# Routing and expert slots in one instruction stream, with the gate's projection turned

## The reference

```python
x = x + tanh(g_xattn[0]) * xattn(ctx, ctx, layernorm(x), ssm_kernel, D, 8)   # long convolution of k*v, then times q
x = x + tanh(g_ffn[0]) * ffn(layernorm(x), G, gate_w, up_w, down_w, lora_A, lora_B)

# ffn
scores = softmax(x @ G)                       # 8 experts
value, indices = top_k(scores, 2)             # w: weight per token and expert, zero but for two
gated = silu(x @ gate_w[e].T) * (x @ up_w[e].T)
out  = sum_e w[e] * (gated @ down_w[e].T)
out += sum_e w[e] * ((x @ lora_A[e].T) @ lora_B[e].T)
```

## Time and profile before

| what | value |
|---|---|
| median of 3 runs | 1526.3 us |
| the three runs | 1525.24 to 1528.57 us |
| profiled execution, its own time | 1529.94 us |
| profiled execution, its span | 1527.8 us |
| mean granted clock | 0.964 |
| busy: TensorE, VectorE, GpSimd, ScalarE | 93%, 75%, 73%, 51% |

### The profile page before, as it was taken

How to read it: one execution, slowest core, us unless ns; L and a number is a source line. 1 busy time by engine, 2 the same in 40 slices (tenths; PEclk the granted TensorE clock), 3 DMA queues, 4 the chain that set the end, 5 groups by cost and what they waited for, 6 DMA issues and landing times. The chain is left out here.

```text
span 1527.8 us, 34088 instructions
## 1 busy us (share of the span) xinstructions
PE 1417.1 (93%) x10482; PEld 1380.8 (90%) x10483; DVE 1151.5 (75%) x1923; ACT 774.4 (51%) x1359; POOL 1113.6 (73%) x982
## 2 busy tenths in 40 slices
PE   3999999999999999999999999933699999999994
PEld 3999999999999999999999999933699999999994
DVE  2999999999999999999999999948245454444542
ACT  5555665666566665656565666310233343433331
POOL 6998988898898989898989898405155555555552
PEclk9999999999999999999999999955799999999998
DMA  6666676767676767676767676345389999999984
GB/s 198 196 220 221 208 222 208 226 203 234 202 221 205 238 196 228 200 232 202 227 200 226 208 219 214 131 158 125 88 180 271 239 238 239 259 263 219 245 172 79
DMA packets 114343, 315.46 MB, mean 206 GB/s; under 512 B 25152, under 2 KB 25664, under 8 KB 114304
## 3 DMA queue, kind: packets, MB, share of 16 engines
q1 hardware_dynamic: 93728, 239.96, 50.2%
q0 software_dynamic: 20576, 75.04, 22.1%
HBM read 215.66 MB, written 100.86 MB: 207 GB/s over the span
## 5 line engine op out<-in xcount | busy, mean ns | idle before, releaser
L532 DVE TENSOR_REDUCE oT<-z 128x128 f32<-128x1280 f32 x256 | 380.4, 1486 | 7.8
L633 PE MATMUL Y<-kvhi,t_hi 128*128 128x288 f32 x1280 | 383.1, 299 | 0.0
L634 PE MATMUL Y<-kvlo,t_hi 128*128 128x288 f32 x1280 | 378.4, 296 | 0.0
L635 PE MATMUL Y<-kvhi,t_lo 128*128 128x288 f32 x1280 | 377.6, 295 | 0.0
L307 POOL TENSOR_TENSOR kvlo<-kv,kvhi 128x1152 fp32r<-128x1152 f32 x128 | 340.6, 2684 | 0.0
L290 POOL TENSOR_TENSOR kv<-cT 128x768 f32<-128x768 f32 x128 | 238.0, 1859 | 9.3 <-DMA cT<-in_c 9.3
L635 PEld LDWEIGHTS Y<-kvhi,t_lo 128*128 128x128 f32 x1280 | 241.4, 189 | 0.0
L634 PEld LDWEIGHTS Y<-kvlo,t_hi 128*128 128x128 f32 x1280 | 241.3, 189 | 0.0
L633 PEld LDWEIGHTS Y<-kvhi,t_hi 128*128 128x128 f32 x1280 | 241.1, 188 | 0.0
L515 DVE TENSOR_TENSOR z<-Y,qT 128x512 f32<-128x512 f32 x256 | 176.9, 691 | 51.2 <-PE Y L635 42.4
L1230 PE MATMUL GU<-wt_hi,xu_hi 128*128 x568 | 171.5, 302 | 0.0
(11 more groups left out here) (172 smaller groups left out, 3402.8 us busy)
## 6 DMA issues: line engine op xcount, KB each, us to landing
cT<-in_c SPq DMA_DIRECT2D x32, 768.0 KB, 8.0
t_hi<-khi SPq DMA_DIRECT2D x64, 384.0 KB, 3.6
t_lo<-klo SPq DMA_DIRECT2D x64, 384.0 KB, 5.0
u_hi<-kshi SPq DMA_DIRECT2D x64, 320.0 KB, 5.8
u_lo<-kslo SPq DMA_DIRECT2D x64, 320.0 KB, 6.9
x_nat<-in_x SPq DMA_DIRECT2D x32, 512.0 KB, 4.1
out<-x_new SPq DMA_DIRECT2D x32, 512.0 KB, 4.8
normed<-n SPq DMA_DIRECT2D x32, 512.0 KB, 7.5
```

What stands on the lines that cost most here:

```text
L532: nc.vector.tensor_reduce(oT[p][:, 2 * r:2 * r + 2, h * IB:(h + 1) * IB], view(z[s][:], [[ZC, 2], [2, IB], [2 * IB, ZS], [1, 2]]), AX.XY, ...
L633: nc.tensor.matmul(out, w_hi[:, w], m_hi[:, c, :], start=start, stop=False)
L634: nc.tensor.matmul(out, w_hi[:, w], m_lo[:, c, :], start=False, stop=False)
L635: return nc.tensor.matmul(out, w_lo[:, w], m_hi[:, c, :], start=False, stop=stop)
```

## The change

- In `attend` the projection is turned: `ag_parts` (16 columns) is the loaded operand and the tile's high and low parts side by side (`n2_parts`, 256 columns) move, 8 matmuls in place of 16. The result lies on 16 partitions. ScalarE copies 16 x 256 of it into `gated` (zeroed once by VectorE), TensorE transposes it back in two matmuls (`turn`, new, between `shared(i, 1)` and `conv(i, 1, 0)`) into XP's second bank, and VectorE sums four numbers for each logit. `take_lr` moves behind `total(i, p, 0, 3)`.
- In the slots HT is gone; `turn` writes into GU of the slot's parity. This frees a bank, so that the PSUM and SBUF tensors of routing and of slots exist together.
- Routing and slots are one `Block`, one program per engine. In place of the stop come the semaphores `spare_out` and `tables_done`.
- In routing the memsets of `lora_b` and `wt` move from VectorE to GpSimd, those of `shift` to where VectorE waits for the counts. `keep.token` and `keep.dest` are formed before the `need` tables; VectorE then waits until GpSimd has issued two gathers (`first_rows`), and makes the tables. SyncE waits for the weights of expert 0 before it issues those of expert 1, and no longer waits for a memset first.
- `lora_b` gets a semaphore of its own, so TensorE waits for two counts in each slot, both computed from the slot's expert in registers.

```diff
                 def take_small(i):
                     eng.wait_ge(ag_ready, i + 1)
-                        eng.wait_ge(lr_done, i)
-                    nc.scalar.copy(p_small[:], XP[:, E:2 * E]).then_inc(small_done, 1)
+                    if isinstance(i, int) and i < 1:
+                        eng.wait_ge(gated_zero, 1)
+                    else:
+                        eng.wait_ge(turned, i)
+                    nc.scalar.copy(gated[0:2 * E, :], XP[0:2 * E, 0:2 * P]).then_inc(small_done, 1)
...
                 def take_lr(i):
-                    eng.wait_ge(ag_ready, i + 1)
+                    eng.wait_ge(turned, i + 1)
-                    eng.wait_ge(small_done, i + 1)
-                    nc.vector.tensor_tensor(to, XP[:, 0:E], p_small[:], ALU.add).then_inc(lr_done, 1)
+                    nc.vector.tensor_reduce(to, view(XP[:], [[1, E], [P, 2], [E, 2]], HALF), AX.XY, ALU.add).then_inc(lr_done, 1)
...
                     multiply(i, p, 0, 3)
+                    total(i, p, 0, 3)
                     if not (isinstance(i, int) and i < 2):
                         take_lr(i - 2)
-                    total(i, p, 0, 3)
...
                     for c in range(NC):
-                        nc.tensor.matmul(XP[:, 0:2 * E], n2_hi[:, c, :], ag_parts[:, c].rearrange("p o n -> p (o n)"),
-                                         start=c == 0, stop=False)
-                        mm = nc.tensor.matmul(XP[:, 0:E], n2_lo[:, c, :], ag_parts[:, c, 0, :], start=False, stop=c == NC - 1)
+                        mm = nc.tensor.matmul(XP[0:2 * E, 0:2 * P], ag_parts[:, c].rearrange("p o n -> p (o n)"),
+                                              n2_parts[:, c].rearrange("p o n -> p (o n)"), start=c == 0, stop=c == NC - 1)
                     mm.then_inc(ag_ready, 1)
+
+                def turn(i):
+                    eng.wait_ge(small_done, i + 1)
+                    for half in range(2):
+                        mm = nc.tensor.transpose(XP[:, HALF + half * P:HALF + (half + 1) * P],
+                                                 gated[:, half * P:(half + 1) * P], ident[:])
+                    mm.then_inc(turned, 1)
...
                     shared(i, 1)
+                    if not (isinstance(i, int) and i < 2):
+                        turn(i - 2)
                     conv(i, 1, 0)
...
@@ route_tokens, VectorE @@
-                V.memset(weights.lb[:].bitcast(F32), 0.0).then_inc(weights.lb_zero, 1)
-                link(V.memset(wt[:], 0.0))
-                for b in range(NB):
-                    link(V.memset(shift[:, b, :], float(NB - 1 - b)))
...
         link(V.memset(cum[:], 0.0))
+        for b in range(NB):
+            link(V.memset(shift[:, b, :], float(NB - 1 - b)))
         eng.wait_ge(cnt_done, 1)
...
+        eng.wait_ge(idx_done, 1)
+        V.tensor_scalar(keep.token[:], IDX[:, 0:SG], -1.0, 0.0, ALU.add, ALU.max).then_inc(token_done, 1)
+        link(V.tensor_scalar(spare[:], IDX[:, 0:SG], 0.0, number[:, NT:NT + 1], ALU.is_equal, ALU.mult))
+        V.scalar_tensor_tensor(out=keep.dest[:], in0=IDX[:, 0:SG], scalar=-1.0, in1=spare[:], op0=ALU.add,
+                               op1=ALU.add)
+        eng.wait_ge(first_rows, 1)
         link(V.tensor_tensor(last[:], ended[:, :, E - 1:E].rearrange("p s o -> p (s o)"), grid[:], ALU.mult))
...
-        V.tensor_scalar(keep.need[:], need_i[:], 16.0, 16.0, ALU.mult, ALU.add)
-        eng.wait_ge(idx_done, 1)
+        V.tensor_scalar(keep.need[:], need_i[:], 16.0, 16.0, ALU.mult, ALU.add).then_inc(keep.tables_done, 1)
...
@@ route_tokens, SyncE @@
-                eng.wait_ge(weights.lb_zero, 1)
                 eng.dma_start(spare_d, normed_d[0:P, 0:L]).then_inc(spare_out, 16)
                 for e in range(2):
                     weights.load(eng, whi_d, wlo_d, e)
+            eng.wait_ge(weights.landed, LANDED * e + LANDED)
+        eng.wait_ge(weights.lb_zero, 1)
                 eng.wait_ge(rt, at["weights"])
...
@@ route_tokens, GpSimd @@
+        nc.gpsimd.memset(weights.lb[:].bitcast(F32), 0.0).then_inc(weights.lb_zero, 1)
+        nc.gpsimd.memset(wt[:], 0.0).then_inc(zeros, 1)
...
         for k in range(NB):
             rows.gather(eng, keep, normed_d, k)
+            if k == 1:
+                nc.gpsimd.memset(issued[:], 0.0).then_inc(first_rows, 1)
...
@@ experts_on_slots @@
-        HT = ps("HT", [P, HALF])
...
+        eng.wait_ge(keep.spare_out, 16)
+        eng.wait_ge(keep.tables_done, 1)
...
             eng.wait_ge(weights.landed, LANDED * e + LANDED)
+            eng.wait_ge(weights.lb_landed, 48 * e + 48)
...
-                    nc.tensor.transpose(HT[:, 0:P], h[p][:, 0:F], ident[:])
-                    nc.tensor.transpose(HT[:, P:2 * P], h[p][:, F:2 * F], ident[:]).then_inc(ht_ready, 1)
+            nc.tensor.transpose(GU[p][:, 0:P], h[p][:, 0:F], ident[:])
+            nc.tensor.transpose(GU[p][:, P:2 * P], h[p][:, F:2 * F], ident[:]).then_inc(ht_ready, 1)
...
+        eng.wait_ge(keep.tables_done, 1)
         read_table(0, 0)
...
@@ build @@
+        with nc.Block() as block:
+            @block.vector
+            def _(eng):
+                route[3](eng)
+                slots[3](eng)
...
```

More of the change, by code:

```diff
@@ L60 @@
 GT = 4
-LANDED = 32 * NT // E + 48
+LANDED = 32 * NT // E
 SLOTS = 2 * TOKENS // P + E - 1
@@ L122, in attend @@
         n2 = [sb(f"n2{p}", [P, L]) for p in range(2)]
-        n2_hi, n2_lo = sb("n2_hi", [P, NC, P], F32R), sb("n2_lo", [P, NC, P], F32R)
+        n2_parts = sb("n2_parts", [P, NC, 2, P], F32R)
         ag = sb("ag", [P, NC, E])
-        p_small = sb("p_small", [P, E])
+        gated = sb("gated", [P, 2 * P])
         ag_parts = sb("ag_parts", [P, NC, 2, E], F32R)
@@ L179, in attend @@
         lr_done = sem("lr_done")
+        turned = sem("turned")
+        gated_zero = sem("gated_zero")
         w_in, whi_done, wlo_done, w_out = sem("w_in"), sem("whi_done"), sem("wlo_done"), sem("w_out")
@@ L442, in high_n2 @@
                         eng.wait_ge(ag_ready, i)
-                    nc.scalar.copy(n2_hi[:], XP[:].rearrange("p (c n) -> p c n", c=NC)).then_inc(n2hi_done, 1)
+                    nc.scalar.copy(n2_parts[:, :, 0, :], XP[:].rearrange("p (c n) -> p c n", c=NC)).then_inc(n2hi_done, 1)
                 def take_small(i):
                     eng.wait_ge(ag_ready, i + 1)
-                    if not (isinstance(i, int) and i < 1):
-                        eng.wait_ge(lr_done, i)
-                    nc.scalar.copy(p_small[:], XP[:, E:2 * E]).then_inc(small_done, 1)
+                    if isinstance(i, int) and i < 1:
[3 more added lines that the diff above has]
+                    nc.scalar.copy(gated[0:2 * E, :], XP[0:2 * E, 0:2 * P]).then_inc(small_done, 1)
                 eng.wait_ge(k_sum, 1)
@@ L746, in _ @@
                 project(NT - 2)
+                turn(NT - 2)
                 transpose_n2(NT - 1, 1)
                 project(NT - 1)
+                turn(NT - 1)
 class Chosen:
@@ L775, in __init__ @@
         self.lb_zero = ctx.enter_context(nc.semaphore("lb_zero"))
+        self.lb_landed = ctx.enter_context(nc.semaphore("lb_landed"))
         self.packed = ctx.enter_context(nc.semaphore("packed"))
@@ L787, in load_b @@
         for n, d in enumerate((bhi_d, bhi_d, blo_d)):
-            eng.dma_start(self.lb[n * ST:n * ST + R, e % 2, :].bitcast(F32), d[e]).then_inc(self.landed, 16)
+            eng.dma_start(self.lb[n * ST:n * ST + R, e % 2, :].bitcast(F32), d[e]).then_inc(self.lb_landed, 16)
     def load(self, eng, whi_d, wlo_d, e, singly=False):
         if singly:
-            eng.wait_ge(self.landed, LANDED * e + 48)
+            eng.wait_ge(self.lb_landed, 48 * e + 48)
         for q in range(NT // E):
@@ L798, in load @@
             if singly:
-                eng.wait_ge(self.landed, LANDED * e + 48 + 32 * (q + 1))
+                eng.wait_ge(self.landed, LANDED * e + 32 * (q + 1))
 class Rows:
@@ L1312, in build, with _ @@
         keep, weights, rows = Chosen(nc, ctx), Weights(nc, ctx), Rows(nc, ctx)
-        route_tokens(nc, keep, weights, rows, logits, constants, normed, whi, wlo, bhi, blo,
-                     normed.rearrange("(t p) l -> p t l", p=P)[:, :, L:RW], out[NT])
-        experts_on_slots(nc, keep, constants, weights, rows, whi, wlo, bhi, blo, normed,
-                         out.rearrange("t p l -> (t p) l"))
+        with ExitStack() as route_ctx:
+            route = route_tokens(nc, route_ctx, keep, weights, rows, logits, constants, normed, whi, wlo, bhi, blo,
+                                 normed.rearrange("(t p) l -> p t l", p=P)[:, :, L:RW], out[NT])
+        slots = experts_on_slots(nc, ctx, keep, constants, weights, rows, whi, wlo, bhi, blo, normed,
+                                 out.rearrange("t p l -> (t p) l"))
+        with nc.Block() as block:
[3 more added lines that the diff above has]
+                slots[3](eng)
+            @block.sync
+            def _(eng):
+                route[0](eng)
+                slots[0](eng)
```

(12 more changed lines are left out.)

826 lines of the change are left out of this document (407 added, 419 removed).

## The result

| what | before | after |
|---|---|---|
| median | 1526.11 us | 1500.16 us |
| lowest and highest of four runs | 1525.24 to 1528.57 us | 1499.49 to 1501.47 us |
| profiled execution, its own time | 1529.94 us | 1499.49 us |
| profiled execution, its span | 1527.8 us | 1497.7 us |

The ratio is 0.9828, with a 95% interval of 0.9811 to 0.9846, that is, 26.0 us less. Forecast were 28 less (1498.5, with 1490 to 1510 as the range).

What follows compares the result with a forecast made beforehand. TensorE bounds attend (VectorE 7% behind) and the slots; between them a chain over VectorE, GpSimd and a stop. 15 + 2.0 + 3.1 + 2.3 + 5.5 = 28 us, median 1526.3 to 1498.5; range 1490 to 1510, from terms' bounds 1494 to 1503.

Steps and rivals of the forecast that it cites:

- Part 1: Turned projection in attend's 30 tiles: 0.5 us saved a tile (0.35 to 0.6), 15 us in all (10.5 to 18).
- an edge of 0 to 0.15: Attend, ahead of `transpose_n2`: TensorE arrives about when the logit reduction is handed over, a stall of 0 to 0.15 us.
- the dearer rival at 1509: Attend: array runs empty when operand width changes, or VectorE's reduction comes later; 0.35 saved a tile, 1509 us; chance 0.13.
- Part 2: End of attend at the lower clock: both last projections on the chain get shorter, 2.0 us saved (1.3 to 2.8).
- Part 3: Head of routing: VectorE's memsets ahead of the first operation on the logits go, 3.1 us saved.
- The contention that I took at 0 (bound 1.9): Head of routing: GpSimd's memsets beside VectorE could slow VectorE, bounds 0 to 1.9 us, taken as 0.
- Part 4: Routing: `keep.token` formed ahead of the tables, straight behind the last IDX matmuls, 2.3 us saved.
- Part 5: Stop between routing and slots removed: token list to first slot transposes 7.6 us for 13.1, 5.5 saved (3.5 to 6.5).
- Part 6: Slots: HT's place in GU and the second wait for weights add no time, cost 0.
- The seam keeps its cost (1504): Rival, routing to slots: TensorE starts no sooner after the token list than now, Part 5 gives 0, 1504 us; chance 0.1.
- The clock comes back sooner (1494.5): Rival, first two slots: shorter TensorE idling lets them run partly at full rate, 4 us more, 1494.5 us; chance 0.1.

Runs made afterwards that it cites:

- bank alone: Kernel before, with only the slots' second transposes written into the bank of their own gate (GU) instead of HT: 1527.13 us, ratio 0.9993.
- tripled waits: Changed kernel with each slot's two waits for weights made three times over, counts computed from the expert's register each time: 1501.23 us, ratio 0.9826 to the kernel before.
- projection alone: Kernel before with the attend of the changed kernel, routing and slots untouched: 1510.37 us, ratio 0.9877.
- no wait for gathers: Changed kernel without VectorE's wait for the first two gathers (`first_rows`) ahead of the tables: 1498.71 us, ratio 0.9815 to the kernel before.
- all three: Changed kernel with logit reduction ahead of `total`, no wait for the gathers ahead of the tables, and function tables loaded early: 1491.69 us, ratio 0.9765 to the kernel before.
- reduction ahead of the sum: Changed kernel with the logit reduction (`take_lr`) put back ahead of `total(i, p, 0, 3)`: 1496.8 us, ratio 0.9791 to the kernel before.
- one program alone: Changed kernel with the attend of the kernel before: 1517.3 us, ratio 0.9923 to the kernel before.
- stop kept: Changed kernel with routing and slots as two blocks again, with the stop of all engines between them: 1508.34 us, ratio 0.9862 to the kernel before.
- tables first: Changed kernel with the need tables again ahead of the token list and without the wait for two gathers: 1501.64 us, ratio 0.9831 to the kernel before.
- memsets on VectorE: Changed kernel with the memsets of `lora_b` and `wt` back on VectorE ahead of the logits' first reduction: 1504.51 us, ratio 0.9847 to the kernel before.
- early tables: Changed kernel with an extra one-column exp in attend and silu in routing, loading ScalarE's function tables early: 1498.81 us, ratio 0.9813 to the kernel before.

## Why the prediction was right, point by point

- **Part 1, 15 us; it was 13.1.** The turned matmuls were priced right (0.119 forecast, 0.117 measured; 0.84 saved forecast, 0.85 measured), the turn a little high (0.28, it was 0.22). The term that was mis-sized is the stall ahead of `transpose_n2`: the prediction called it an edge of 0 to 0.15 and took 0.5 out of 0.56 a tile; by the list of waits it is 0.21. Counted from the start of the projection, the prediction had TensorE at the transposes after 6.81 and the reduction's end after 6.69; they were 6.74 (608.29 + 0.13) and 6.76. Each was off by 0.07, and together with the hand-over of 0.15 that makes the stall. Here the two engines meet within 0.02 us, so the stall is the hand-over, and it should have been priced, not bounded. The run with the order turned gave it back, 5.6 / 30 = 0.19 a tile.
- **The drain (the dearer rival at 1509) is refuted.** A 16-column operand between 128-column ones showed neither a gap ahead nor behind: 0.13 from the last turned matmul's stream to the second convolution matmul. By the rule of the Trainium skill (TensorEngine Tiling (Array Packing), Tiling Modes, Key Properties) a change of mode would drain TensorE. The trace shows no drain at either change of width, so this operand either isn't another mode or costs nothing as one; no run tells the two apart.
- **Part 2, 2.0; it was 2.1.** From the start of the last projection to the turn it is 2.34 where 2.46 was forecast.
- **Part 3, 3.1; it was 3.2**, with two errors that cancel. Gone were 3.6, since VectorE also entered its program 0.4 sooner after the logits; but I didn't ask what the memsets had been covering on a third engine. ScalarE's table load was, and 0.34 came back. The contention that I took at 0 (bound 1.9) was 0.
- **Part 4, 2.3, and Part 5, 5.5; they were 2.4 and 5.2.** Each is right as an interval between two rows, but they aren't two gains that add, and in this the prediction's sum is right by its accounting and not by its mechanism. From the logits to the first transposes, with 3.2 taken off for the head of routing in the kernel before, it is 59.3 with the stop and the tables first, 57.3 with the stop and the list first, 51.7 without the stop in either order. What is real is 7.6 in all. Taking out the stop gives all of it, or 5.5 if the order has given its 2.0 already; the order, with its wait for the gathers, gives nothing once the stop is gone. In the tables path the step from the last table to TensorE was 1.07, not 0.7.
- **Part 6, 0; it was 0**, by two runs, the bank alone and the tripled waits.
- **The seam keeps its cost (1504)** is refuted by the rows: 7.96, not 13.1. What the engines did in those 13 us is settled in part only: 5.5 of it goes with the stop. Whether it is instructions that come in or the engines' meeting itself no run tells.
- **The clock comes back sooner (1494.5).** It did in the profiled execution. From the first transposes to those three slots on it took 1066.52 - 1048.16 = 18.4 where it was 21.1 before. But this is no property of the change. TensorE's granted clock rises to 1.00 in slot 0 or 1, and in seven of the thirteen profiled executions it falls once more to 0.50 in slot 1. The same distance with one rise: 18.4, 18.8 (projection alone), 18.3 (no wait for gathers), 18.3 (tripled waits), 18.1 (all three). With a second fall: 21.1 (before), 21.0 (reduction ahead of the sum), 21.1 (one program alone), 21.1 (stop kept), 21.3 (tables first), 20.8 (memsets on VectorE), 21.0 (bank alone). With the early tables it was 17.1, 1.3 of the difference being the table. The second fall, in the table of stretches of the run with the reduction ahead of the sum (the changed kernel has 1.00 from 1056 on, as its row of 1060 to 1076 above):

```profile
1051.00:1054.00 3.00, 2.33 (x14) 2.10 (x13) 0.13 (x3) 0.62 (x2) 0.94 (x1) 0.80 0.21 22
1054.00:1057.00 3.00, 1.47 (x7) 1.47 (x8) 0.66 (x3) 1.51 (x3) 0.00 (x0) 0.77 0.41 155
1057.00:1060.00 3.00, 3.00 (x19) 3.00 (x18) 1.24 (x2) 1.01 (x1) 0.00 (x0) 0.66 0.00 0
```

Two things go with the fall. One is the moment of the first rise: it came 7.3 to 8.6 us behind the first transposes in five executions, and none of them fell again; it came 9.5 to 10.5 behind them in the other eight, and seven fell. The other is TensorE's idle time ahead of slot 0's transposes of h, behind the rise: 2.20 while ScalarE loads the silu's table, 0.79 with the early tables. The one late rise without a fall is the run of all three together, which has the 0.79. Its rows, with the same transposes in the run with the reduction ahead of the sum first:

```profile
1055.53 0.43 PE L1268 MATMUL GU<-const_ident,h 128*128 128x128 f32 x1 [2.20 <-DVE h L1200]
```

```profile
1052.74 0.33 PE L1271 MATMUL GU<-const_ident,h 128*128 128x128 f32 x1 [0.79 <-DVE h L1203]
```

```profile
1049.00:1051.00 2.00, 2.00 (x11) 2.00 (x10) 0.68 (x3) 0.00 (x0) 0.52 (x1) 0.52 0.00 0
1051.00:1054.00 3.00, 2.21 (x19) 1.99 (x18) 0.66 (x3) 0.75 (x3) 0.41 (x1) 1.00 0.58 168
```

So the early tables may also keep the clock from falling when it rises late; with one such execution that is not shown. The projection alone has the seam of before and the short form, the stop kept and the tables first have the new attend and the long one, so the form is not set by the change. The mean granted clock of single runs points the same way: of 29 executions of the kernel before beside the experiments, the nine up to 1527.2 us had 0.965 or 0.966, the others 0.963 to 0.965. The rival was right that 2.7 us lie here, and wrong in what would win them; what decides when the clock first rises stays open.

The terms were off by -1.9, +0.1, +0.1, +0.1, -0.3, so 26.0 came in place of 28, and 1500.2 in place of 1498.5, inside the forecast's own range of 1494 to 1503. The upper end of that range is not the sum of the bounds: the least saving of each part adds up to 20.7, which is 1505.6. The result lies inside either way. That the errors of Parts 2 to 5 are so small is partly luck, as said of Part 3 and of Parts 4 and 5. The choice to work against the profiled execution's own time and to come back to the median was needed: the executions start their first tile up to 2 us apart, and the first slots differ by 2.7 with the clock.

## What to carry to other kernels

When work is moved off a chain, read what every other engine did under it, for what was covered, here a function table load, comes to light as soon as the cover is gone. Two edits at one join are no sum: price each path from its fork to the join, and look at which ends last. Here moving the tables from before the fork to behind it was worth 2.0 with the stop, nothing without it as long as they waited for the gathers, and 1.8 without that wait. A reduction that frees a shared PSUM bank belongs ahead of a longer one that nobody waits for; two instructions in the wrong order were a fifth of the gain here.

## What the runs showed of the hardware

- Loading 16 columns and moving 256 costs 0.117 us a matmul at the higher clock, and a 16-column operand's load 0.094 against 0.19 for 128 columns; switching between the two cost nothing (0.13 from matmul to matmul ahead and behind).
- A stop of all engines between two programs cost 5.5 us with the list first (13.5 from the token list to the slots with it, 8.0 without, with 5.62 of idle VectorE behind its last table) and 7.6 with the tables first (59.3 against 51.7 from the logits to the slots).
- A memset of 2048 columns on GpSimd (1.80) beside VectorE's reductions of 256 columns didn't slow them (0.42 each); tables on VectorE beside GpSimd's gathers slowed the gathers' issue from 1.02 to 1.41 and from 0.97 to 1.19.
- The clock's return after the idle stretch has two forms, 2.7 us apart, in executions of nearly the same program: a rise 7.3 to 8.6 us behind the first transposes that holds, or one 9.5 to 10.5 behind them that was followed by a second fall in seven of eight executions.
- A one-column exp or silu issued long before took the table load of 1.28 off the chain: 0.34 came back at the exp and 1.3 at the first silu, no more than the load itself.
